# Criss-cross attention on one core: from the third row chunk on, GpSimd scales the softmax weights block by block into turned places and VectorE turns the blocks; loads and first-batch work are issued a step earlier

## The reference

```python
q = einsum('oc,bchw->bohw', Wq, x) + bq      # 64 channels
k = einsum('oc,bchw->bohw', Wk, x) + bk      # 64 channels
v = einsum('oc,bchw->bohw', Wv, x) + bv      # 512 channels
energy_H = einsum('bchw,bcgw->bhwg', q, k) - 1e30 * eye   # along the column, itself left out
energy_W = einsum('bchw,bchv->bhwv', q, k)                # along the row
att = softmax(concat([energy_H, energy_W], -1))
out = gamma * (einsum('bcgw,bhwg->bchw', v, att_H) + einsum('bchv,bhwv->bchw', v, att_W)) + x
```

## Time and profile before

| what | value |
|---|---|
| median of 3 runs | 4036.08 us (4032.39 to 4038.2) |
| the profiled execution | 4029.24 us, span 4027.5 us |
| mean granted TensorE clock | 0.981 |
| busy share PE, VectorE, ScalarE, GpSimd | 96%, 60%, 41%, 16% |

### The profile page before, as it was taken

How to read it: one execution, slowest core, us unless ns; L and a number is a source line. 1 busy time by engine, 2 the same in 40 slices (tenths; PEclk the granted TensorE clock), 3 DMA queues, 4 the chain that set the end, 5 groups by cost and what they waited for, 6 DMA issues and landing times.

```text
span 4027.5 us, 72644 instructions
## 1 busy us (share of the span) xinstructions
PE 3864.0 (96%) x28440; PEld 3830.9 (95%) x28440; DVE 2433.0 (60%) x5084; ACT 1663.7 (41%) x3658; POOL 627.1 (16%) x793
## 2 busy tenths in 40 slices
PE   5679999999999999999999999999999999999999
PEld 5579999999999999999999999999999999999999
DVE  4544668456674577745676466754668457673554
ACT  4442445424454244433444334542445424444111
POOL 0131003210032001310023100221003210042000
PEclk7789999999999999999999999999999999999999
DMA  4277775967768776677767777687775877758665
GB/s 165 85 201 219 236 254 185 242 219 241 233 198 227 232 243 226 203 217 239 245 213 213 217 245 251 198 226 219 238 251 186 234 220 236 242 186 226 202 200 173
DMA packets 256803, 874.33 MB, mean 217 GB/s; under 512 B 34256, under 2 KB 108496, under 8 KB 256464
## 3 DMA queue, kind: packets, MB, share of 16 engines
q1 hardware_dynamic: 256464, 869.67, 70.2%
HBM read 661.92 MB, written 207.62 MB: 216 GB/s over the span
## 4 chain that ended last, share of the span: by engine, by line
PE 90%; DMA 4%; DVE 4%; issue 1%; ACT 0%; POOL 0%; SPq 0%; DVEq 0%; ACTq 0%; POOLq 0%
PE bank L910 39%; PE bank L898 17%; PE bank L879 14%; PE bank L828 11%; DMA Pe<-e_scratch 4%; PE bank L838 3%; PE bank L865 3%; PE bank L847 3%; DVE E L629 1%; DVE mx L624 1%; DVE Sx L610 1%; DVE zs L638 0%; POOL Pe L390 0%; DMA XA<-in_x 0%; DVE Sy L615 0%
## 5 line engine op out<-in xcount | busy, mean ns | idle before, releaser
L910 PE MATMUL bank<-Sy,Wv_hi 128*128 128x384 f32 x6144 | 1596.1, 340 | 11.9 <-DVE Sy L615 11.9
L910 PEld LDWEIGHTS bank<-Sy,Wv_hi 128*128 128x128 f32 x6144 | 1088.3, 188 | 13.1 <-issue 13.1
L910 PE MATMUL bank<-Sy,Wv_lo 128*128 128x384 f32 x3072 | 1029.1, 335 | 0.0
L695 DVE SCALAR_TENSOR_TENSOR Y<-bank,bv_sb,Y 128x384 f32<-128x384 f32 x768 | 472.0, 615 | 871.7 <-PE bank L910 871.2
L390 POOL TENSOR_TENSOR Pe<-Pe,F 96x384 f32<-96x384 f32 x384 | 321.6, 840 | 2681.6 <-DMA Pe<-e_scratch 2647.7
L898 PE MATMUL bank<-Pt,XT_r 128*128 128x96 f32 x6144 | 724.8, 275 | 8.0 <-ACT Y L505 6.2
L898 PEld LDWEIGHTS bank<-Pt,XT_r 128*128 128x128 f32 x6144 | 705.0, 192 | 10.7 <-issue 7.6
L516 ACT ACTIVATE Sy<-Y 128x768 fp32r<-128x768 f32 x384 | 303.0, 836 | 896.6 <-PE bank L910 861.8
L678 DVE COPY Y<-bank 128x96 f32<-128x96 f32 x1536 | 317.5, 320 | 493.4 <-PE bank L879 493.4
L910 PEld LDWEIGHTS bank<-Sy,Wv_lo 128*128 128x128 f32 x3072 | 577.1, 188 | 0.0
L505 ACT ACTIVATE Y<-bank 128x96 f32<-128x96 f32 x1536 | 321.5, 359 | 395.1 <-PE bank L879 395.1
(11 more groups left out here) (62 smaller groups left out, 3298.0 us busy)
## 6 DMA issues: line engine op xcount, KB each, us to landing
Y<-in_x SPq DMA_DIRECT2D x192, 768.0 KB, 6.0
XT_r<-in_x_row SPq DMA_DIRECT2D x384, 384.0 KB, 5.4
out<-Y SPq DMA_DIRECT2D x192, 768.0 KB, 3.6
XA<-in_x SPq DMA_DIRECT2D x180, 768.0 KB, 6.9
XT_r<-in_x_col SPq DMA_DIRECT2D x192, 384.0 KB, 5.1
XT_c<-in_x_col SPq DMA_DIRECT2D x192, 384.0 KB, 5.1
e_scratch<-E SPq DMA_DIRECT2D x384, 144.0 KB, 2.7
Pe<-e_scratch SPq DMA_DIRECT2D x384, 144.0 KB, 7.0
```

Source lines behind the costliest of these rows:

```text
L695: nc.vector.scalar_tensor_tensor(at, proj_ps[c % 2][:, 0:CP], bv_sb[:, c:c + 1], at, op0=ALU.add, op1=ALU.add).then_inc(out_made, 1)
L910: last = nc.tensor.matmul(proj_ps[c % 2][:, 0:CP], w[:, ct, at], Sy[:, lo, ct, :], start=(ct == 0 and k == 0), stop=(ct == CT - 1 and k == 2))
```

## The change

Chunks 0 to 25 of a batch (`BY_PE = 26`: all columns and the first two row chunks) go as before. Chunks 26 to 47 no longer touch TensorE, PSUM or ScalarE. GpSimd writes nine products of 32 partitions x 4 rows x 32 columns, block (h, g) of `Pe` to block (g, h) of `Pt`. VectorE then transposes each 32 x 32 block in place. That is 22 chunks in each of 8 batches. Four other things move: in the prologue `round_x` and `low_x` run two chunks ahead of `project_kq` instead of one; in the column stage `load_p` is issued one step earlier; the load of x for the residual of chunk 0 (`load_xres(b, 0)`) moves from the middle of the column stage to the start of the row stage; for batch 0 the first x columns are loaded in the prologue's row part and `first_loads` stands at its 8th, not 12th, column group.

```diff
+BY_PE = CHUNKS + 2
...
             def load_p(b, i):
                 along, n = i // CHUNKS, i % CHUNKS
-                sp.wait_ge(p_turned, past(p_turned, p_no(b, i - PRING)))
+                if PRING <= i < BY_PE + PRING:
+                    sp.wait_ge(p_turned, past(p_turned, pt_no(b, i - PRING)))
+                else:
+                    sp.wait_ge(p_scaled, past(p_scaled, p_no(b, i - PRING)))
...
                 for g in range(CHUNKS):
-                    if g:
-                        load_p(b, g + PRING)
+                    load_p(b, g + PRING + 1)
...
-                    if g == CHUNKS // 2:
-                        load_xres(b, 0)
 
             def row_stage(b, more):
-                load_p(b, CHUNKS + 3)
                 load_xtr(b, 3)
+                load_xres(b, 0)
...
+            def scale(b, i, masked=0):
...
+                pool.wait_ge(o_summed, past(o_summed, o_no(b, (i - 2) * ROWS + ROWS - 1)))
+                pool.wait_ge(p_scaled, past(p_scaled, p_no(b, i - 1)))
+                pool.wait_ge(c_masked, past(c_masked, (b + 1) * CHUNKS + masked))
+                to = Pt[:, i % 2, :].rearrange("p (r n) -> p r n", r=ROWS)
+                for h in range(0, N, BLOCK):
+                    for g in range(0, N, BLOCK):
+                        last = nc.gpsimd.tensor_tensor(
+                            to[g:g + BLOCK, :, h:h + BLOCK], Pe[h:h + BLOCK, i % PRING, :, g:g + BLOCK],
+                            f[h:h + BLOCK, :, :].to_broadcast((BLOCK, ROWS, BLOCK)), ALU.mult)
+                last.then_inc(p_scaled, 1)
...
             def row_stage(b, more):
-                scale(b, CHUNKS + 3)
                 for n in range(CHUNKS):
+                    if n + 3 < CHUNKS and not (more and b_groups(n)):
+                        scale(b, CHUNKS + n + 3)
...
-                    for g in b_now[:3]:
+                    for g in b_now:
                         if g + 2 < CHUNKS:
                             gather_k(b + 1, g + 2)
                         mask(b + 1, g)
-                    if n + 4 < CHUNKS:
-                        scale(b, CHUNKS + n + 4)
...
+                        if g == b_now[0] and n + 3 < CHUNKS:
+                            scale(b, CHUNKS + n + 3, g + 1)
...
-                    if n + 3 < CHUNKS:
-                        copy_turned(b, CHUNKS + n + 3)
...
                 round_x(0, 0)
+                round_x(0, 1)
...
-                    if m + 1 < CHUNKS:
-                        round_x(0, m + 1)
                     evict_kq(0, m, before=False)
+                    if m + 2 < CHUNKS:
+                        round_x(0, m + 2)
...
+            def turn(b, i):
+                dve.wait_ge(p_scaled, past(p_scaled, p_no(b, i)))
+                at = Pt[0:N, i % 2, :]
+                nc.vector.transpose(at, at).then_inc(ptr_made, 1)
...
                     if a_now:
                         sum_z(b + 1, a_now[0])
+                    if n + 3 < CHUNKS:
+                        turn(b, CHUNKS + n + 3)
                     finish(b, n, 2)
...
                 low_x(0, 0)
+                low_x(0, 1)
                 for m in range(CHUNKS):
-                    if m + 1 < CHUNKS:
-                        low_x(0, m + 1)
+                    if m + 2 < CHUNKS:
+                        low_x(0, m + 2)
...
-                    if n + 3 < CHUNKS:
-                        turn(b, CHUNKS + n + 3)
```

More of the change, by code:

```diff
@@ L25 @@
 RBANKS = 3
+BLOCK = 32
+BY_PE = CHUNKS + 2
 A_FIRST, A_LAST = 6, 17
@@ L178, in p_no, with pt_no, ptr_no, weights_turned @@
             return b * (2 * CHUNKS) + i + 1
+        def pt_no(b, i):
+            return b * BY_PE + i + 1
+        def ptr_no(b, i):
+            return b * (2 * CHUNKS - BY_PE) + i - BY_PE + 1
+        def weights_turned(eng, b, i):
+            if i < BY_PE:
+                eng.wait_ge(pt_made, past(pt_made, pt_no(b, i)))
+            else:
+                eng.wait_ge(ptr_made, past(ptr_made, ptr_no(b, i)))
         def o_no(b, i):
@@ L264, in first_loads @@
             def first_loads(b):
-                for i in range(RRING):
-                    load_xtc(b, i)
+                if b:
+                    for i in range(RRING):
+                        load_xtc(b, i)
                 for i in range(PRING):
@@ L415, in row_stage @@
                         mask(b + 1, g)
-                    if n + 4 < CHUNKS:
-                        scale(b, CHUNKS + n + 4)
-                    for g in b_now[3:]:
-                        if g + 2 < CHUNKS:
-                            gather_k(b + 1, g + 2)
-                        mask(b + 1, g)
+                        if g == b_now[0] and n + 3 < CHUNKS:
+                            scale(b, CHUNKS + n + 3, g + 1)
             def prologue():
@@ L716, in row_stage @@
                 add_row(b, 1, 3)
+                turn(b, CHUNKS + 2)
                 for n in range(CHUNKS):
@@ L721, in row_stage @@
                     finish(b, n, 0)
+                    if more and n + 1 == A_FIRST:
+                        low_x(b + 1, 0)
                     if b_now and b_now[0]:
@@ L744, in row_stage @@
                         shift(b + 1, a_now[1])
-                    if more and n + 1 == A_FIRST:
-                        low_x(b + 1, 0)
                     if b_now:
@@ L926, in row_stage @@
                 for n in range(2):
-                    turn(b, CHUNKS + n + 1)
+                    if n == 0:
+                        turn(b, CHUNKS + 1)
                     for r in range(ROWS):
```

31 lines of the change are left out of this document (18 added, 13 removed).

## The result

The changed kernel takes 3904.64 us (median of 4 runs, 3900.14 to 3905.59) against 4034.35 us for the kernel before (median of 4 runs; the three shown ahead of the change have 4036.08): a ratio of 0.9675, interval 0.9658 to 0.9692. Forecast were 3885 us and 3845 to 3935. The time is inside the range, 20 us above the forecast. The forecast set -26 us for the moved turns, -81 for the prologue and -44 for the column stages. In the two profiled executions, whose spans differ by 124.6 us, they are **+15** (what is left for the row stages), -91.5 and -48 us; by the medians of runs that take the edits out, +19, -95 and -56. Moving the turns, which gives the change its name, cost time; the edits that came with it won all of the gain.

A forecast was written before the change was run, and what follows sets the result against it. The prediction took TensorE, busy 96% of the span, to bound the kernel. Its terms -26 - 81 - 44 = -151 us took the profiled 4029 to 3878, plus 7 for the median: 3885 us, range 3845 to 3935.

The forecast's parts named there:

- Term 1: Row stages: 176 turns off TensorE save 58 us, VectorE's waiting for GpSimd costs 32, net -26 us.
- Plain steps: Row steps without next-batch projection or column groups: each loses its 0.33 us turn, 12.26 to 11.93 us.
- A steps: Row steps that project the next batch: the 0.33 us turn goes and its replacement costs nothing.
- Cost nothing: Plain row steps and those projecting the next batch: products and transpose hide behind TensorE's work, at no cost.
- B steps: Row steps with column groups: in 18 to 20, VectorE waits 2 us for GpSimd; 17.2 us against TensorE's 15.43.
- fixed cost per block: Rival: no fixed GpSimd time overlaps, so nine block products take 4.1 us, total 3904 us; chance 0.15.
- Term 2: Prologue: two-chunk look-ahead cuts a chunk from 7.1 to 3.7 us at nearly full clock, -81 us in all.
- lower clock: Rival: the prologue stays at the lower clock, 5.5 us a chunk, 40 us less gain, 3925 us; chance 0.09.
- Term 3: Column stages: earlier weight requests and the moved `Y` load remove stalls and half-rate time, -44 us.
- bound by transfers: Rival: in column stages only stalls behind the mid-stage `Y` load go, -15 us, total 3914 us; chance 0.08.
- The signs named beforehand: Expected profile after: shorter plain steps, VectorE waiting in steps 18 to 20, faster prologue, 95 us column stages.

The follow-up runs named there:

- e1: The changed kernel with all turns back on TensorE and ScalarE's copy, prologue and load edits kept: 3885.25 us, ratio 0.9627.
- e3: The changed kernel with VectorE's sum of the first attended row moved ahead of the first low part of `Sy` in every row step: 3864.18 us, ratio 0.9575.
- e13: The changed kernel with all turns on TensorE and the first attended row's sum ahead of the low part: 3884.79 us, ratio 0.9633.
- e7: The changed kernel with each GpSimd product writing to the 32 partitions it reads, so blocks stand wrong: 3886.24 us, one run.
- e4: The changed kernel with VectorE's turn placed behind the attended-row sums in row steps with column groups: 3871.99 us, ratio 0.9594.
- e8: The changed kernel with the load of the first residual (`Y`) back in the middle of the column stage: 3902.35 us, ratio 0.9676.
- e2: The kernel before with only the prologue's two-chunk look-ahead added: 3941.20 us, ratio 0.9765.
- e11: The changed kernel with the two loops over blocks exchanged, so three products in a row write the same partitions: 3905.26 us, ratio 0.9682.
- e5: The changed kernel, in steps with column groups: VectorE's turn behind the sums, nine products in three lots behind the first three masks: 3846.67 us, ratio 0.9537.

## Why the prediction was right, and where it was wrong

**The total.** Right in its range and near in its value, and that is in part luck, for the errors partly cancel: the prologue gave 10 to 14 us more than forecast, the columns 4 to 12 more, the turns 45 less. The forecast had the sign of its first term wrong. One sum of the prediction is slightly off: products of 1.3 us a block give 3885 + 21 x 8.5 = 4064, not 4066.

**Term 1, the turns.** Forecast -58 + 32 = -26; measured +19 (e1), and +15 by what the traces leave for the row stages (+17 against e1). In pieces, over all batches, from the steps of the traces:

- *Plain steps*, 63 of them: -0.33 each forecast, -0.32 found. Right.
- *A steps*, 84: -0.33 each forecast, -28 us; found -0.15 (-0.32 in the first of each batch), some -14 us. The failed step is "Cost nothing" for A steps, which was argued from a plain step (VectorE busy 6.23 of 12.26 us) and from where the transpose stands. It asked whether what is added is hidden, and not what the time taken out had hidden itself: the chain to the fourth attended row (e3, e13).
- *B steps*, 21 with a turn: forecast +32 - 7 = +25; found 6.3 to 7.9 us per batch, +50. The mechanism was right, to the engine and the place: VectorE waits before the transpose and TensorE then for `add_row`. Two sizes were off. The nine products take 3.99 us and not 3.2: this is the rival *fixed cost per block*, whose 4.1 us is met almost exactly. And a microsecond of products costs more than the 21 us of the forecast: in e7 (one run) 0.55 us fewer gave 18 us, 33 per microsecond. By that price the missing 25 us are 0.79 x 33 = 26. The clock, which the forecast left at full, is at half for 3.4 us once per batch behind the wait. It doesn't explain the 33, for it is so in the seven batches of e7 too. But it is a cost in itself: the one batch of e7 in which it lasts twice as long has B steps 1.3 us longer in sum than the others, which makes an estimate of 9 us in seven batches, and 0.79 x 21 + 9 = 26 us as well. The runs don't tell the two accounts apart. The account was short on GpSimd's side too: the prediction named what is queued behind VectorE's wait, and not the masks that are queued behind the nine products (e4: 56.9 us of waits for them).
- *The first two row chunks*: 7.47 before, less a turn should be 7.14; found 7.4 to 7.9, 4 us more in all. The load of `Y` at the start of the row stage makes 3 of them, where 2 were put down (e8: 7.2 to 7.5 without it).

The rule of the Trainium skill cited beside that rival (page "GPSIMD Engine Reference", section "Elementwise — side-by-side cycle accounting") is borne out in its direction: 128 elements on 32 partitions take 0.39 us and 384 on 96 take 0.82, so by the elements a partition 128 are worth 0.215 us and 0.175 is fixed, as by the select of the earlier trace rows. I had granted that part of it overlaps. From start to start it is even more than the 0.39 where partitions change (0.45), and a little less where they don't (0.36, e7).

**Term 2, the prologue.** Forecast -81, found -91.5 in the trace and -95 with e2. Mechanism and clock right (1.00). The chunk was put at 3.7 us, above VectorE's own 3.4, without a row for the 0.3 between them. It is 3.3 (start to start of a chunk's matmuls):

```profile
40.02 0.59 PE L867 MATMUL bank<-Sx_first,Wqk_hi 128*128 128x384 f32 x2 [0.29 <-DVE Sx_first L640]
...
43.33 0.59 PE L867 MATMUL bank<-Sx,Wqk_hi 128*128 128x384 f32 x2 [0.32 <-DVE Sx L640]
```

The 2.72 us of waiting in the earlier trace rows became 0.3. VectorE is busy 67.87 of 70.24 us in this part, so it binds at its own time, with no gap to add; ScalarE, with 67.36, is close to the same limit. 22 x 0.4 = 9 us, which is what the row part gave beyond its 77; the column part of the prologue gave 5, where the wait of the earlier trace rows had been put down with 4.4, and that wait is gone. The rival *lower clock* was wrong.

**Term 3, the columns.** Forecast -44, of which -46 in the stages; found -48.4 in the traces, and 48 to 56 between e2 and e1. Right in size, and in that the waits for `Pe` went. TensorE's wait for the scaled weights, before at its turn and now (the few that are left stand at L904, the turn of the changed kernel):

```profile
PE bank L865 <- POOL Pe L390: 31.9, 22, 3.1
```

```profile
PE bank L904 <- POOL Pe L413: 1.5, 3, 0.7
```

Of its two causes the first was enough: with the earlier request for weights, the load of `Y` in mid-stage does next to nothing (e8). The rival *bound by transfers* held that only the stalls behind that load would go, and fell: those at the start of the stage went too. What stays is 2.9 us of idle time in all eight stages, where 5 were put down for the stalls on x.

**The signs named beforehand.** Plain steps at 11.93: yes. B steps 18 to 20 above 15.76 with VectorE waiting for GpSimd: yes. Steps 21 and 22 below: no, 15.40 to 16.4 and 12.79 against 15.40 and 12.79; TensorE had no turn there to lose. Row part of the prologue ending near 100 us: earlier, at 88.64. Column stages of 95 us (93.4 to 95.9) without waits for `Pe`: yes, to 1.5 us.

## What to carry to other kernels

When work is taken off the engine that binds, ask what that work had covered: the next chain may have less slack than was removed, and the profile marks no wait while the removed work still stands there. A block of instructions that fits an engine's total time can still be too long in one piece; cut it to the gaps between what others wait for, and look at everything queued behind it on its own engine as well as on the engine that waits. And undo each edit alone: this change was 3.2% faster with one of its three terms pulling the other way, and the same edits in another order are 5.1% faster.

## What the runs showed of the hardware

- Short GpSimd products (32 partitions, 128 elements each) take 0.39 us, and follow each other by 0.45 us when the partitions read or written change, by 0.36 us when neither does (e7, e11). Nine cost 3.99 us, nearly five of the whole products of 0.82 us that they replace.
- The block transpose of 96x384 on VectorE takes 0.57 us, as long as a reduction of the same tile (0.54).
- VectorE's subtraction of two SBUF operands (L645) takes 0.95 us, but 1.44 at 563.29 in the timeline above, where GpSimd's copy `Kg` (L388) had begun before it and runs beside it for 0.62 us. Over all 384:

```profile
L645 DVE TENSOR_TENSOR Sy<-Y,Sy x384: 941/949/1454, 245.8 to 3888.1; 128x768 fp32r<-128x768 f32 x192
```

  Where the subtraction begins first, the copy is the longer one, 1.46 us where its median is 0.87:

```profile
598.47 0.95 DVE L645 TENSOR_TENSOR Sy<-Y,Sy 128x768 fp32r<-128x768 f32 x1
598.66 1.46 POOL L388 COPY Kg<-KQ 64x384 f32<-64x384 f32 x1 [2.14 <-PE bank L886]
```

  The trace of the changed kernel has it so throughout. The 333 subtractions with no GpSimd instruction beside them take 0.94 to 0.96 us. The 14 that begin during a copy and share 0.60 to 0.63 us with it take 1.43 to 1.45, and those copies keep 0.83 to 0.86. The 14 that begin before a copy keep 0.95 to 0.96, and those copies take 1.46 to 1.58. So whoever begins second pays. The sum of an attended row (L721), which has one operand in PSUM, takes 0.54 to 0.56 us with or without GpSimd beside it.

  The Trainium skill, page "SBUF — State Buffer", section "Who interferes with whom", says that VectorE and GpSimd share a pair of ports under an exclusive lock. The rows agree in that one hinders the other; of 0.62 us side by side the subtraction loses 0.49.
- TensorE's granted clock fell to half for 3.4 us where it had just stood idle for 2.7 us in the B step (565.25 in the timeline: eight narrow matmuls in 2.02 us, against 0.93 by e3's row). That is 1.2 in place of 2.4 GHz. It did so once in each of seven batches, three times behind the wait in step 19 and four times behind that in step 20; four equal waits in step 19 left it at full. In the 21 B steps of e5, without idle time, it stayed at 1.00. A window of the changed kernel:

```profile
565.20:568.30 3.10, 3.05 (x17) 3.05 (x17) 3.00 (x6) 0.52 (x1) 0.03 (x1) 0.50 0.94 279
```
